# A mixture-of-experts stage with the down products two places behind, gate and up in one bank, and the down weights split behind the tanh

## What is computed

```python
logits = x @ gate_w.T
topv, topi = jax.lax.top_k(logits, TOP_K)
rw = jax.nn.softmax(topv.astype(jnp.float32), axis=-1).astype(x.dtype)
W = jnp.zeros((N, E), x.dtype).at[jnp.arange(N)[:, None], topi].set(rw)
gu = jnp.einsum('nh,eih->nei', x, gu_w)
gate, up = (gu[..., :I], gu[..., I:])
inter = jax.nn.silu(gate) * up
inter_w = inter * W[:, :, None]
out = jnp.einsum('nei,ehi->nh', inter_w, dp_w)
...
x = x + jnp.tanh(g_ffn[0]) * _L0_ffn_ref(_layernorm(x, axis=-1), ...)
```

## Time and profile before

| what | us |
|---|---|
| median of three executions | 1693.7 |
| lowest and highest of the three | 1691.89, 1697.5 |
| the profiled execution | 1702.99 |
| its span, first to last instruction | 1701.2 |
| expert stage in the span | about 1170 to 1606 |
| of it the two-tile places | about 1268 to 1605 |
| granted TensorE clock, mean of the span | 0.947 |

### The profile page before, as it was taken

One profiled execution on the slowest core, in us unless ns is written; L12 is line 12 of the kernel. 1 busy time (PEld: TensorE's weight loads), 2 busy tenths in 40 slices (PEclk: granted clock), 3 DMA queues, 4 the chain that ended last, 5 costly groups with the idle time before them and its releaser, 6 DMA issues.

```text
span 1701.2 us, 24871 instructions
## 1 busy us (share of the span) xinstructions
PE 1477.5 (87%) x7674; PEld 1192.3 (70%) x7674; DVE 1117.0 (66%) x2423; ACT 680.8 (40%) x1565; POOL 952.6 (56%) x987
## 2 busy tenths in 40 slices
PE   7998999998999998999999897826888888888974
PEld 5766887776887776787777676615777777777742
DVE  5777780687882588883489747333657666666486
ACT  2333770111770111771011635203656656665520
POOL 4654670376773277674268743245777766666421
PEclk9999999999999999999999999957989999998998
DMA  8888205555104655103654042475788988887597
GB/s 249 300 298 288 69 6 162 182 170 154 31 6 125 194 177 163 41 6 113 191 172 151 16 160 66 149 251 163 213 245 270 290 267 274 262 247 245 183 423 293
DMA packets 164777, 309.01 MB, mean 182 GB/s; under 512 B 38235, under 2 KB 73653, under 8 KB 162805
## 3 DMA queue, kind: packets, MB, share of 16 engines
q1 hardware_dynamic: 132900, 245.42, 43.4%
q0 software_dynamic: 31744, 61.99, 12.6%
HBM read 239.01 MB, written 70.43 MB: 182 GB/s over the span
## 4 chain that ended last, share of the span: by engine, by line
PE 57%; DVE 12%; issue 8%; DMA 8%; ACT 5%; another core or an unknown queue 5%; POOL 3%; SPq 1%; POOLq 0%; DVEq 0%; ACTq 0%
PE bank L698 15%; PE bank L700 14%; PE bank L699 14%; PE bank L798 6%; PE bank L824 3%; DMA p_in<-parts 3%; DVE q_sin L1111 2%; PE bank L961 2%; DVE q_rope L1107 1%; DMA v_w3l<-v_dram 1%; POOL q_rope L1721 1%; ACT prob L1492 1%; ACT y_sb L1629 1%; POOL prob L1727 1%
## 5 line engine op out<-in xcount | busy, mean ns | idle before, releaser
L1721 POOL TENSOR_TENSOR q_rope<-q_rope,q_sin 128x448 f32<-128x448 f32 x192 | 217.9, 1164 | 151.9 <-DVE q_sin L1111 150.9
L1727 POOL TENSOR_TENSOR prob<-prob,row_inv 128x375 f32<-128x375 f32 x209 | 168.7, 813 | 113.8 <-DVE row_inv L1133 111.7
L1802 POOL DMA_INDIRECT parts<-y_sb,t_rows x140 | 150.0, 1071 | 103.6 <-ACT y_sb L1629 70.4
L1795 POOL DMA_INDIRECT x_g<-xn_dram,t_rows x140 | 163.5, 1168 | 52.2 <-issue 41.5
L1742 POOL DMA_INDIRECT table<-entry,pos_i x128 | 125.8, 983 | 88.6 <-DVE count L1221 58.0
L798 PE MATMUL bank<-q_rope,m_w 128*128 128x448 f32 x384 | 159.5, 552 | 13.7 <-DVE q_tl L1117 9.0
L1111 DVE TENSOR_TENSOR q_sin<-bank,sin_q 128x448 f32<-128x448 f32 (+1 forms) x256 | 157.9, 617 | 4.0
L1125 DVE TENSOR_REDUCE row_max<-bank 128x1 f32<-128x375 f32 x224 | 119.4, 534 | 37.1 <-PE bank L700 33.8
L1629 ACT ACTIVATE y_sb<-bank,t_rows 112x512 f32<-112x512 f32 (+5 forms) x140 | 91.4, 688 | 110.6 <-PE bank L700 62.7
L824 PE MATMUL bank<-ident,prob 128*125 128x128 f32 x672 | 115.3, 282 | 19.8 <-POOL prob L1727 9.8
L1492 ACT ACTIVATE prob<-bank,row_max 128x375 f32<-128x375 f32 x224 | 128.4, 574 | 10.0 <-DVE row_max L1125 9.4
(11 more groups left out here) (291 smaller groups left out, 4533.7 us busy)
## 6 DMA issues: line engine op xcount, KB each, us to landing
w_gu<-in_w_gu SPq DMA_DIRECT2D x64, 512.0 KB
p_in<-parts SPq DMA_DIRECT2D x14, 2048.0 KB, 16.8
w_dp<-in_w_dp SPq DMA_DIRECT2D x64, 256.0 KB
m_w<-m_dram SPq DMA_DIRECT2D x48, 192.0 KB, 2.5
wq_s0h<-wq_dram SPq DMA_DIRECT2D x24, 256.0 KB
wq_s0l<-wq_dram SPq DMA_DIRECT2D x24, 256.0 KB
wq_s1h<-wq_dram SPq DMA_DIRECT2D x24, 256.0 KB
wq_s1l<-wq_dram SPq DMA_DIRECT2D x24, 256.0 KB
```

The costliest lines, as they stand in the source:

```text
L1721: pool.tensor_tensor(o[:, c, :], o[:, c, :], q_sin[:, c, :], ALU.add).then_inc(s_radd, 1)
L1727: pool.tensor_tensor(prob[i][:], prob[i][:], row_inv[:, i:i + 1].to_broadcast([P, L]), ALU.mult)\
L1795: pool.indirect_dma_start(x_g[x % NXE][0:size, t, :], None, xn2_dram, bass.IndirectOffsetOnAxis(ap=t_rows[x % NROW][0:size, t, 0:1].bitcas ...
L1802: pool.indirect_dma_start(parts, bass.IndirectOffsetOnAxis(ap=t_rows[x % NROW][0:size, t, 1:2].bitcast(I32), axis=0), y_sb[x % NY][t][0:si ...
```

## The change

Four things are changed, all in the expert stage.

1. `DOWN_LAG = 2`: `down` and `put` come two places behind `inner` instead of one, on PE, ACT and POOL. `e_inner_s` gets a third buffer, and PE's loop one more turn.
2. `gate_up(x)`: a two-tile place puts gate and up into one bank (columns 0 and 256), bank 3 and bank 4 in turn. The gate's start at x then waits for `e_inner` of x - 2, and the tanh waits for gate and up both (`s_gu`). Behind a three-tile place it waits for `e_inner` of x - 1, and a three-tile place still uses banks 3 and 4.
3. `split_expert` is cut in two: `split_gate_up(x + 1)` stays ahead of the inner steps of x, and `split_down(x + 1)` comes behind the tanh on ACT and behind all four inner steps on DVE. The gate's start waits for the first alone, `down` for the second.
4. The down results take banks 5, 6, 7 in turn over all tiles, and each waits for the evacuation three tiles back.

```diff
+SHARED_UP = 256
+DOWN_LAG = 2
+def gate_up(x):
+    return ((3, 0), (4, 0)) if TILES[x][1] == 3 else ((3 + x % 2, 0), (3 + x % 2, SHARED_UP))
...
             def inner(x):
                 cap = CAPS[x]
-                pe.wait_ge(s_ws_v, 2 * (x + 1))
+                pe.wait_ge(s_ws_v, 2 * x + 1)
                 pe.wait_ge(s_et_v, FIRST[x + 1])
-                for bk, at in ((3, 0), (4, I)):
-                    if x:
-                        pe.wait_ge(s_inner, 4 * (x - 1) + (1 if bk == 3 else 2))
+                if x and TILES[x - 1][1] == 3:
+                    pe.wait_ge(s_inner, 4 * (x - 1) + 2)
+                elif x:
+                    pe.wait_ge(s_inner, 4 * (x - 2) + 2)
...
             def down(x):
                 pe.wait_ge(s_inner, 4 * (x + 1))
+                pe.wait_ge(s_ws_v, 2 * x + 2)
                 for t in range(tiles):
-                    if x and t < TILES[x - 1][1]:
-                        pe.wait_ge(s_y, FIRST[x - 1] + t + 1)
+                    n = FIRST[x] + t
+                    if n >= 3:
+                        pe.wait_ge(s_y, n - 2)
...
+            def split_down(x):
                 if x >= 3:
                     act.wait_ge(s_down, FIRST[x - 2])
                 act.activation(w_dp_s[x % 3][0][:], w_dp[x % NE][:], ACT.Copy).then_inc(s_ws_a, 1)
             def inner(x):
-                act.wait_ge(s_gate, x + 1)
+                act.wait_ge(s_gate if TILES[x][1] == 3 else s_gu, x + 1)
...
-            for x in range(E + 1):
+            for x in range(E + DOWN_LAG):
                 if x + 1 < E:
                     turn(x + 1)
-                    split_expert(x + 1)
+                    split_gate_up(x + 1)
                 if x < E:
                     inner(x)
-                if x >= 1:
-                    down(x - 1)
+                if x + 1 < E:
+                    split_down(x + 1)
+                if x >= DOWN_LAG:
+                    down(x - DOWN_LAG)
```

More of the change, by code:

```diff
@@ L337, in build @@
             e_inner = [expert_sb(f"e_inner{i}", [I, CAP]) for i in range(2)]
[L338 removed]
+            e_inner_s = [[expert_sb(f"e_inner_s{i}{p}", [I, CAP], F32R) for p in "hl"] for i in range(3)]
         p_in = [kept(f"p_in{i}", [P, KY, C]) for i in range(NC)]
@@ L1356, in inner @@
                 i, cap = x % 2, CAPS[x]
-                high, low = (t[:, 0:cap] for t in e_inner_s[i])
+                gate, up = (bank[bk][:, col:col + cap] for bk, col in gate_up(x))
+                high, low = (t[:, 0:cap] for t in e_inner_s[x % 3])
                 half, both = e_half[i][:, 0:cap], e_inner[i][:, 0:cap]
                 dve.wait_ge(s_tanh_e, x + 1)
-                dve.scalar_tensor_tensor(half, e_tanh[i][:, 0:cap], 1.0, bank[3][:, 0:cap], ALU.add, ALU.mult)\
+                dve.scalar_tensor_tensor(half, e_tanh[i][:, 0:cap], 1.0, gate, ALU.add, ALU.mult)\
                    .then_inc(s_inner, 1)
@@ L1628, in down @@
                     act.wait_ge(s_down, FIRST[x] + t + 1)
-                    act.activation(y_sb[x % NY][t][0:size, :], bank[5 + t][0:size, :], ACT.Copy,
+                    act.activation(y_sb[x % NY][t][0:size, :], bank[5 + (FIRST[x] + t) % 3][0:size, :], ACT.Copy,
                                    scale=t_rows[x % NROW][0:size, t, 2:3]).then_inc(s_y, 1)
-            split_expert(0)
+            split_gate_up(0)
+            split_down(0)
             turn(0)
-            for x in range(E + 1):
+            for x in range(E + DOWN_LAG):
                 if x + 1 < E:
                     turn(x + 1)
-                    split_expert(x + 1)
+                    split_gate_up(x + 1)
                 if x < E:
                     inner(x)
-                if x >= 1:
-                    down(x - 1)
+                if x + 1 < E:
+                    split_down(x + 1)
+                if x >= DOWN_LAG:
+                    down(x - DOWN_LAG)
             def body(eng, r, x):
@@ L1807, in gpsimd @@
                 gather(x)
-            for x in range(E + 1):
+            for x in range(E + DOWN_LAG):
                 if x + NG_AHEAD < E:
                     gather(x + NG_AHEAD)
-                if x >= 1:
-                    put(x - 1)
+                if x >= DOWN_LAG:
+                    put(x - DOWN_LAG)
             def body(eng, r, x):
```

30 lines of the change are left out of this document (17 added, 13 removed).

## The result

The changed kernel takes 1700.96 us (median of seven executions, 1697.57 to 1703.57), the kernel before, in seven, 1693.53 us. The ratio is 1.0047, with a 95% interval of 1.0029 to 1.0066: it is about 8 us slower, where 10.5 us less had been forecast. The time lies outside the range of 1667 to 1698.

A forecast was written before the change was run, and what follows sets the result against it. PE was taken as nearest to the bound, its gate-start waits as the place to gain. Terms 3.9 + 6 - 2.9 + 2 + 3 - 1.5 = 10.5 us, off the median 1693.7, gave 1683 us; forecast 1677 to 1689, range 1667 to 1698.

The forecast's parts named there:

- the second candidate: POOL's gathers and puts: 5.7 us for a two-tile place, under the 6.5 it takes; bound only in three-tile places.
- it delays nothing: DVE's low split of the down weights, 0.7 us, moved behind the inner steps, ends ahead of ACT's transposes' evacuation.
- kinds A and T: PE's gate-start waits after late transposes (10 waits, 10.3 us) or a late tanh (5, 11.6 us); savings 3.9 and 6 us.
- Kind B: Late evacuation on ACT, PE waiting one place later, 8 waits, 10.65 us; the change makes it 2.9 us worse in all.
- ACT loop rival: ACT's down-weights copy waits for this turn's down products, so ACT's loop sets every place's pace; about 1700 us, chance 0.14.
- Gathers: POOL's gather moves one place ahead against the put, so PE's waits for gathered rows shrink: 2 us (0 to 3).
- Clock: Two or three of ten slow PE stretches become shorter: 3 us of 27 gained (0 to 12).
- Tail: At the stage's end three places' puts remain behind the last up instead of two: 1.5 us lost (0 to 2.5).
- Loads: SP's weight load for x + 3 is issued up to 1.7 us later, 4 to 5 with a late signal; costed at nothing.

The follow-up runs named there:

- again2: The kernel before, unchanged, on a chip without late signals; ratio 1.0004, median 1651.5 us.
- after3: The changed kernel, unchanged, on a chip without late signals; ratio to the kernel before 1.0048, median 1657.6 us.
- early_load: The changed kernel, with the gate and up weights' load waiting for their own low split alone; ratio to the kernel before 1.0024, median 1651.1 us.
- thin loads: Kernel before and changed kernel, each loading 96 KB of weights a place from the fourth place on; ratios to the kernel before 0.9967 and 1.0014.
- lag1: The changed kernel with the down products one place behind instead of two; ratio to the kernel before 1.0036 on the chip with late signals.
- again: The kernel before, unchanged, on the chip with late signals; ratio 0.9998.
- dplater: The changed kernel with down weights split in their own place's turn and gate/up loads waiting for the gate/up split alone; ratios to the kernel before 0.9989 and 0.9932.

## Why the prediction was wrong

*What bounds the kernel.* The working took PE for the bound and looked at its waits at the gate's start. On the chip of the first profile that was where PE waited, and the waits for `e_half` did vanish. But the second candidate was dismissed by a comparison of rates: 5.7 us of POOL for a place against 6.5. Of those 6.5 the late signals and the slow clock are 1.7; once PE has none of them (or works faster through the change), a place takes 4.8 to 4.9 us, and POOL's 5.6 are more. The waits then went to gathered rows: none before in that stretch, 12.5 us after. On the other chips they had been there all along. That is the first step that failed: a stage with two engines within 15% of each other has two bounds. On the first chip POOL was the bound in part only. The pace of the two-tile places stayed at 6.5 us, POOL still waited 38.6 us for `y_sb`, and 12.5 of the 25.2 us that PE waited at the turn were for rows.

*POOL's price as a constant.* The second failed step is the term that was not in the sum. A gather at 1174 ns and a put at 1051 were used as fixed prices, though the last put, with no split of DVE beside it, takes 0.92. Most of the difference was held time (32 us over the stage's 280 gathers and puts in the first profile), and an edit that moves DVE's splits against POOL's instructions changes it. In the sum this stood at nothing; on the chips without late signals POOL's sum came out 5 to 12 us longer than in *again2*, beside a loss of 0.48 to 0.61%. The part on DVE ("it delays nothing") looked at who waits for the split's result and not at who is held while it runs.

*Gate's starts of kinds A and T.* Right in mechanism: PE waits 11.6 us among the gate and up products in place of 36.8. Wrong in worth: most came back as waits at the turn, 25.2 for 8.1. The 9.9 us put down for the two were at most 6 us of PE's waits in all.

*Kind B and the ACT loop rival.* ACT's new wait was as predicted, about 1 us ahead of the copy. On the first chip it stands ahead of 24 of the 42 copies in the two-tile places, 0.93 us each; in *after3* ahead of all 46, 1.02 us each. The loop stayed hidden, as the working had it (5.22 against 5.36 us). Gates 4.92 and 4.91 us apart follow one another without a wait. From the changed kernel, PE's three gate's starts, and the copies on ACT between them:

```profile
1351.30 0.36 PE L705 MATMUL bank<-xg_t0h,w_gu_s0h 128*128 128x240 f32 x1
...
1356.22 0.36 PE L705 MATMUL bank<-xg_t1h,w_gu_s1h 128*128 128x240 f32 x1
...
1361.13 0.36 PE L705 MATMUL bank<-xg_t0h,w_gu_s0h 128*128 128x240 f32 x1
```

```profile
1355.67 0.63 ACT L1633 ACTIVATE w_dp_s1h<-w_dp 128x512 fp32r<-128x512 f32 x1 [0.91 <-PE bank L707]
...
1360.59 0.63 ACT L1633 ACTIVATE w_dp_s2h<-w_dp 128x512 fp32r<-128x512 f32 x1 [1.01 <-PE bank L707]
```

So the slower side came true, but not by the rival that stood for it. PE waits for a gate/up split only twice, 2.7 us.

*Gathers.* The term of +2 us rested on a wrong reading of the order: `put(x - DOWN_LAG)` stands in the turn in which PE makes those products, before and after, so a gather's place against PE's work did not move. Waits for rows grew.

*Clock.* +3 us was forecast; it fell from 0.92 to 0.90.

*Tail.* The last put starts at 1604.64, 10.8 us after the last gate's start at 1593.83; before it was 8.3 us (1605.44 and 1597.1). The cost is 2.5 us, the upper end of what was given.

```profile
1593.83 0.36 PE L705 MATMUL bank<-xg_t1h,w_gu_s1h 128*128 128x192 f32 x1
```

```profile
1604.64 0.92 POOL L1825 DMA_INDIRECT parts<-y_sb,t_rows  x1 [0.30 <-issue]
```

*Loads.* The later loads were costed at nothing. *early_load* gives 7 us back, but its held time falls as well (51.9 to 34.5 us, POOL's sum from 322.7 to 305.0), and with thin loads the gap stays at 9 us. That the gap outlives thin loads speaks for held time more than for lateness; how much of the 7 is which was not told apart.

**What is shown and what is open.** Shown: on chips without late signals POOL bounds the stage, the time follows POOL's sum, and cutting one DVE instruction in four takes most of the held time and the changed kernel's loss away together. Argued only: why the lag and the down split together bring POOL's starts into DVE's splits at these moments, early in the gate/up split and often in that of the inner values. Open: the loss of the first result itself. In its two profiles the held time is 38.8 us after and 32.0 before, about as much apart as the medians, but POOL also had idle time there that could take it up, and on its like *lag1* lost 0.36% with a sum no larger than *again*'s (308.9 and 310.6). Late signals and held instructions mix there, and no set fell on such a chip after the cut was known.

## What to carry to other kernels

Ahead of any reordering, look at the POOL rows by the time at which they start, not by their mean: if the same indirect DMA takes 0.95 and 1.8 us, see what DVE was doing at its start. Where GpSimd is near the bound, keep DVE's instructions that read two SBUF tiles short (four pieces of 1.44 us together instead of one of 1.23 gave 0.7% on the kernel before and 1.4 to 1.9% on the changed one here) and cut before you reorder. And when one engine's waits are removed, compute the pace of the next one at that speed, not at the old pace with the waits in it.

## What was not expected of the hardware

The same program had medians of 1646 to 1650 us on three chips, and of 1694 and 1706 us in the two other places it was timed; on one chip its executions mostly stay within 0.6% of their median. The difference is in the expert stage (385 against 437 us between first and last gate): on the slower ones PE's instructions and the signals of its work came late about every 20 us, on the others never. Why is not known. What an edit is worth can then depend on the chip: *dplater* gave 0.9989 (0.9972 to 1.0007) on one kind and 0.9932 (0.99 to 0.9963) on the other. For lag 1, 1.0036 and 0.9993, the intervals overlap.
